# Attention in four in-order queues: output products in high and low parts, q's copy on ScalarE, and steps of VectorE, ScalarE and GpSimd in another order

## The reference

```
x: (16, 512, 256); 16 heads of 64; windows of 128 tokens, 4 in a sequence
qkv = x @ w_qkv;  q, k = l2norm(q) * q_scale * 8, l2norm(k) * k_scale
q, k rotated by position (cos, sin)
each window attends to itself, the one before and the one after
sim = where(mask, -max, q k^T);  attn = softmax(sim);  out = attn v
y = layernorm(x + out @ w_out)
```

## Time and profile before

| | |
|---|---|
| median of 3 runs | 3100.35 us (3098.9 to 3100.77) |
| the profiled execution | 3097.64 us, its span 3095.8 us |
| PE busy | 2941.9 us (95% of the span) |
| DVE busy | 2357.9 us (76%) |
| ACT busy | 2162.1 us (70%) |
| POOL busy | 1662.0 us (54%) |
| masked scores, VectorE, 1024 | 529.7 us |
| exps, ScalarE, 1024 | 572.0 us |
| output products, TensorE, 1024 records | 228.0 us |

### The profile page before, as it was taken

The page is one execution under the profiler, slowest core; times in us unless marked ns, Lnnn a source line. Parts: engine busy times, 40 slices in busy tenths (PEclk is TensorE's granted clock), DMA queues, the critical chain, the costliest instruction groups (busy, mean ns, idle before and its releaser), DMA issues. The chain is left out here.

```text
span 3095.8 us, 60269 instructions
## 1 busy us (share of the span) xinstructions
PE 2941.9 (95%) x20143; PEld 2332.4 (75%) x20143; DVE 2357.9 (76%) x6845; ACT 2162.1 (70%) x5670; POOL 1662.0 (54%) x2226
## 2 busy tenths in 40 slices
PE   7999999999999999999999996799999999999996
PEld 5777777777777777777777774578888888888885
DVE  6877877877877877877877875787777777777775
ACT  5666766766766766766766764577888888888884
POOL 5655655655655655655655654344555555555555
PEclk9999999999999999999999998899999999999998
DMA  2000000000000000000000002100000000000000
GB/s 84 8 15 22 8 15 22 8 15 22 8 15 17 13 15 15 15 15 15 15 15 15 8 21 64 47 15 8 15 15 15 21 20 16 15 15 15 8 15 21
DMA packets 51218, 57.50 MB, mean 19 GB/s; under 512 B 3008, under 2 KB 48592, under 8 KB 50912
## 3 DMA queue, kind: packets, MB, share of 16 engines
q1 hardware_dynamic: 47904, 50.67, 5.1%
q10 hardware_dynamic: 3008, 2.98, 0.3%
HBM read 36.86 MB, written 16.78 MB: 17 GB/s over the span
## 5 line engine op out<-in xcount | busy, mean ns | idle before, releaser
L627 POOL TENSOR_SCALAR a_ex<-a_ex,a_rc 128x384 f32<-128x384 f32 (+1 forms) x1024 | 533.8, 536 | 691.4 <-DVE a_rc L538 691.2
L433 ACT ACTIVATE a_ex<-a_sm,a_nm 128x384 f32<-128x384 f32 (+1 forms) x1024 | 572.0, 560 | 72.5 <-DVE a_nm L531 61.2
L531 DVE CUSTOM_DVE_ANT_0 a_sm<-sc,a_mask,a_rn 128x384 f32<-128x384 f32 (+1 forms) x1024 | 529.7, 543 | 6.3 <-PE sc L303 6.3
L439 ACT ACTIVATE a_pt<-tp 128x256 f32<-128x256 f32 (+1 forms) x512 | 220.1, 430 | 290.5 <-PE tp L322 290.5
L267 PE MATMUL pj<-a_whi,a_xhi 128*128 128x384 f32 x1024 | 390.3, 381 | 8.8 <-DVE a_wlo L187 5.8
L1695 POOL TENSOR_TENSOR b_alo<-b_ring,b_ahi 128x512 fp32r<-128x512 f32 x128 | 169.6, 1325 | 411.7 <-DVE b_ring L1524 388.0
L611 POOL TENSOR_TENSOR a_qr<-a_ra,a_rb 128x256 f32<-128x256 f32 x512 | 370.5, 739 | 11.2 <-DVE a_rb L511 8.4
L267 PE MATMUL pj<-a_whi,a_xlo 128*128 128x384 f32 x1024 | 347.4, 339 | 0.0
L267 PE MATMUL pj<-a_wlo,a_xhi 128*128 128x384 f32 x1024 | 346.3, 338 | 0.0
L331 PE MATMUL qk<-a_pt,a_v 128*64 128x384 f32 (+1 forms) x2048 | 303.9, 437 | 29.0 <-DVE a_pt L543 26.8
L303 PE MATMUL sc<-a_kT,a_qT 64*64 64x256 f32 (+1 forms) x4096 | 307.6, 415 | 1.6 <-DVE a_nm L531 0.9
(11 more groups left out here) (234 smaller groups left out, 7988.7 us busy)
## 6 DMA issues: line engine op xcount, KB each, us to landing
a_xres<-x SPq DMA_DIRECT2D x16, 512.0 KB, 3.8
y<-a_res SPq DMA_DIRECT2D x16, 512.0 KB, 2.9
b_y<-y SPq DMA_DIRECT2D x16, 512.0 KB, 3.8
a_xin<-x SPq DMA_DIRECT2D x15, 512.0 KB, 3.8
out<-b_y SPq DMA_DIRECT2D x15, 512.0 KB, 2.9
a_xin<-wqkv SPq DMA_DIRECT2D x8, 256.0 KB, 2.7
a_ot<-wqkv ACTq DMA_DIRECT2D x3, 384.0 KB, 9.8
a_stage<-wqkv SPq DMA_DIRECT2D x3, 384.0 KB, 12.3
```

What stands on the lines that cost most here:

```text
L433: e.activation(ex[h][w][:, 0:width], sm[h][w % 2][:, 0:width], ACT.Exp, bias=nm[:, w, h:h + 1], scale=-1.0, accum_out=rs[:, w, h:h + 1]).t ...
L439: e.activation(pt_window(0, w), blocks(TP, w), ACT.Copy).then_inc(g['pt_act'], 1)
L531: e.tensor_tensor_reduce(out=sm[h][w % 2][:, 0:width], in0=SC[w % 2][h][:, 0:width], in1=mem['mask'][:, off:off + width], scale=rn[:, par, ...
L627: e.tensor_scalar(row, row, 0.0, rc[:, w, h:h + 1], ALU.add, ALU.mult).then_inc(g['exn_pool'], 1)
```

## The change

The transposed output of attention, `ot`, and its weights `wo` (fp32) become pairs of a high and a low part in the type fp32r: `ohi` is ScalarE's copy of the value products, `olo` is VectorE's difference between these and `ohi`; `wo_hi` and `wo_lo` are made in the first sequence. Each output product becomes three. TensorE's q transposes, which overwrite the bank, wait for `olo`. q's copy goes from VectorE to ScalarE. Masked scores are written straight to `ex`. On TensorE, q's transposes come after the first weights' transposes and half of a projection, and k's after those of window 1's first head. On VectorE, in half u = 1 of pairs 1 to 5 and 7, the last copy of weights and the rotation of chunk 2 come ahead of the last masked score, and the reciprocal of window 1 goes into the next half, behind the rotation of chunk 3. The second statistics go to the end of (1, 0), the power to the end of (1, 1). The residual's x is loaded into `res` itself, so that transfer waits for the maxima and the store. The diff, cut to its core:

```diff
@@ pe_q_transpose, pe_k_transpose, pe_transpose_weights (h and spare)
-            e.wait_ge(g['ot_act'], n)
+            e.wait_ge(g['ol_dve'], n)
-        e.wait_ge(g['qt_dve'], m + 1)
+        e.wait_ge(g['qt_act'], m + 1)
@@ pe_values
-        e.wait_ge(g['pt_act'], NW * n + NW)
-        e.wait_ge(g['pt_dve'], NW * n + NW)
         for k in range(NW):
+            if k in (0, 2):
+                e.wait_ge(g['pt_act'], NW * n + NW - 1 + k // 2)
+                e.wait_ge(g['pt_dve'], NW * n + (NW if k or spare(NW * n + NW - 1) else NW - 1))
@@ pe_out_project
             for c in range(HC):
-                last = e.matmul(QK[:, t * DIM:(t + 1) * DIM], ot[:, c, ...],
-                    wo[:, c, :], start=c == 0, stop=c == HC - 1)
+                for j, (rows_t, weight) in enumerate(((ohi, wo_hi), (olo, wo_hi), (ohi, wo_lo))):
+                    last = e.matmul(QK[:, t * DIM:(t + 1) * DIM], rows_t[:, c, tokens], weight[:, c, :],
+                        start=c == 0 and j == 0, stop=c == HC - 1 and j == 2)
@@ pe_half, u == 0
-            if at.has_pair(1):
-                pe_q_transpose(e, n, n + 1, (p + 1) % 2)
             pe_transpose_weights(e, i, w, 0, at.has_next())
             if at.has_pair(2):
                 pe_project(e, seq, n + 2, pair, w, 0)
+            if at.has_pair(1):
+                pe_q_transpose(e, n, n + 1, (p + 1) % 2)
+            if at.has_pair(2):
                 pe_project(e, seq, n + 2, pair, w, 1)
             pe_transpose_weights(e, i, w, 1, at.has_next())
+            pe_transpose_weights(e, i + 1, w + 1, 0, at.has_next())
             if at.has_pair(1):
                 pe_k_transpose(e, n + 1, (p + 1) % 2)
-            pe_transpose_weights(e, i + 1, w + 1, 0, at.has_next())
@@ act_half, u == 0
+            act_evacuate_weights(e, i, w)
             if ahead:
                 act_exp(e, next_i, next_w, 0)
-            act_evacuate_weights(e, i, w)
+            if at.has_pair(1):
+                act_q_evacuate(e, n + 1, (p + 1) % 2)
             if ahead:
                 act_exp(e, next_i, next_w, 1)
                 act_exp(e, next_i + 1, next_w + 1, 0)
             if at.has_pair(2):
                 act_project(e, n + 2, (p + 2) % PAIRS, w)
+            act_evacuate_weights(e, i + 1, w + 1)
             if at.has_pair(1):
                 act_k_evacuate(e, n + 1, (p + 1) % 2)
-            act_evacuate_weights(e, i + 1, w + 1)
@@ act_half, u == 1
                 act_exp(e, next_i, next_w, 0)
+            if at.has_pair(2):
+                act_project(e, n + 2, (p + 2) % PAIRS, w)
...
                 act_exp(e, next_i + 1, next_w + 1, 1)
-            if at.has_pair(2):
-                act_project(e, n + 2, (p + 2) % PAIRS, w)
+        if at.first and (at.at(3, 1) or at.at(5, 1)):
+            act_out_weights(e, p // 4)
@@ new on VectorE
+    def dve_o_low(e, n, p):
+        e.wait_ge(g['ot_act'], n + 1)
+        e.tensor_tensor(olo[:, p, :], QK[:, :], ohi[:, p, :].bitcast(F32), ALU.subtract).then_inc(g['ol_dve'], 1)
@@ dve_half
             dve_rotate(e, n + 1, 3)
+        if u == 0 and i and spare(i - 1):
+            dve_reciprocals(e, i + 1, w + 1)
+        if u == 0 and at.has_pair(1):
             dve_norms(e, n + 1)
         if u == 1 and at.has_pair(2):
             dve_rotate(e, n + 2, 1)
-        if not at.first:
-            if at.at(1, 0):
-                dve_stats(e, at.b - 1, 1)
+        if u == 0 and at.has_pair(-1):
+            dve_o_low(e, n - 1, (p - 1) % PAIRS)
...
-        if u == 0 and at.has_pair(1):
-            dve_q_evacuate(e, n + 1, (p + 1) % 2)
...
         dve_evacuate_weights(e, i, w)
+        if ahead and u == 1 and spare(i + 1):
+            dve_evacuate_weights(e, i + 1, w + 1)
+            if at.has_pair(2):
+                dve_rotate(e, n + 2, w)
+            dve_mask_max(e, next_i + 1, par, next_w + 1, 1)
+            dve_reciprocals(e, next_i, next_w)
+        else:
+            (as before: masked score, reciprocal, statistics and residual, copy;
+             then for u == 0 the rotation ahead of the second reciprocal)
+        if at.at(1, 0) and not at.first:
+            dve_stats(e, at.b - 1, 1)
@@ pool_half
             pool_rotate(e, n + 2, p % 2, w)
-        if at.at(1, 0) and not at.first:
+        if at.at(1, 1) and not at.first:
             norm.rstd(e, at.b - 1)
+        if at.first and p in (4, 6):
+            pool_out_weights(e, p // 6, u)
@@ SP
             def keep(seq):
-                e.wait_ge(g['op_dve'], 2 * seq)
-                e.dma_start(mem['xres'][:, :, :], x_tiles[seq]).then_inc(g['x_keep'], 16)
+                if seq:
+                    e.wait_ge(g['am_dve'], seq)
+                    e.wait_ge(g['y_out'], 16 * seq)
+                else:
+                    e.wait_ge(g['wo_pool'], 4)
+                e.dma_start(mem['res'][:, :, :], x_tiles[seq]).then_inc(g['x_keep'], 16)
             for b in range(B - 2):
                 load(b + 2)
+                store(b)
                 keep(b + 1)
-                store(b)
```

More of the change, by code:

```diff
@@ L167, in run_attention, with dma_out_weights, act_out_weights, pool_out_weights @@
     w_in = [nc.alloc_semaphore(f'att_w_in{k}') for k in range(len(PIECES))]
-    w_raw = [mem['stage'][:, :], flat(mem['ot'])[:, 0:3 * HD]]
+    w_raw = [mem['raw'][:, c, :] for c in range(DC)]
     def piece_columns(k):
         return slice(PIECES[k][0] * 3 * PW, (PIECES[k][-1] + 1) * 3 * PW)
-    RAW_UNDER = {0: 3, 3: 4, 4: 5}
+    wo_raw = flat(mem['res'])
+    wo_split = [t[:, :, :].rearrange('p c n -> p (c n)') for t in (wo_hi, wo_lo)]
+    def dma_out_weights(e, k):
+        e.dma_start(mem['res'][:, :, :], io['wo0'].rearrange('(c p) n -> p c n', p=P)[:,
+            4 * k:4 * k + 4, :]).then_inc(g['wo_in'], 16)
+    def act_out_weights(e, k):
+        e.wait_ge(g['wo_in'], 16 * (k + 1))
+        e.activation(wo_split[0][:, k * 1024:(k + 1) * 1024], wo_raw, ACT.Copy).then_inc(g['wo_act'], 1)
+    def pool_out_weights(e, k, part):
+        e.wait_ge(g['wo_act'], k + 1)
+        cols = slice(k * 1024 + part * 512, k * 1024 + (part + 1) * 512)
+        e.tensor_tensor(wo_split[1][:, cols], wo_raw[:, part * 512:(part + 1) * 512],
+            wo_split[0][:, cols].bitcast(F32), ALU.subtract).then_inc(g['wo_pool'], 1)
     x_first = [nc.alloc_semaphore(f'att_x_first{k}') for k in range(2)]
@@ L486, in act_half @@
                 act_exp(e, next_i, next_w, 0)
+            if at.has_pair(2):
+                act_project(e, n + 2, (p + 2) % PAIRS, w)
+            if ahead:
                 act_exp(e, next_i, next_w, 1)
@@ L528, in dve_mask_max @@
         e.wait_ge(g['sc_pe'], 2 * i + h + 1)
-        if due(2 * i + h - 3):
-            e.wait_ge(g['e_act'], 2 * i + h - 3)
-        e.tensor_tensor_reduce(out=sm[h][w % 2][:, 0:width], in0=SC[w % 2][h][:, 0:width],
+        e.tensor_tensor_reduce(out=ex[h][w][:, 0:width], in0=SC[w % 2][h][:, 0:width],
             in1=mem['mask'][:, off:off + width], scale=rn[:, par,
@@ L560, in dve_amax @@
         col = TT * seq + t
-        e.tensor_reduce(mem['amax'][:, col:col + 1], mem['res'][:, t, :], AX.X, ALU.max, apply_absolute_value=True)
+        last = e.tensor_reduce(mem['amax'][:, col:col + 1], mem['res'][:, t, :], AX.X, ALU.max,
+            apply_absolute_value=True)
+        if t == TT - 1:
+            last.then_inc(g['am_dve'], 1)
     def dve_half(e, at):
@@ L680, in _ @@
                 e.wait_ge(signal, 16 * DC)
-            e.dma_start(mem['wo'][:, :, :], io['wo0'].rearrange('(c p) n -> p c n', p=P)).then_inc(g['wo_in'], 16)
-            e.dma_start(mem['xres'][:, :, :], x_tiles[0]).then_inc(g['x_keep'], 16)
             load(1)
+            e.wait_ge(g['trig_dve'], 1)
+            dma_out_weights(e, 0)
+            e.wait_ge(g['wo_pool'], 2)
+            dma_out_weights(e, 1)
+            keep(0)
             for b in range(B - 2):
                 load(b + 2)
+                store(b)
                 keep(b + 1)
-                store(b)
-            keep(B - 1)
-            store(B - 2)
             e.wait_ge(g['xt_pe'], 2 * B)
@@ L692, in _ @@
             for k in range(W1_COUNT):
+                if k == 2:
+                    store(B - 2)
+                    keep(B - 1)
                 if k >= 2:
@@ L736, in _ @@
             act_norms(e, 0, 0)
-            for t in range(TT - 1):
+            for t in range(2):
                 act_project(e, 1, 1, t)
+            act_q_evacuate(e, 0, 0)
+            act_project(e, 1, 1, 2)
             act_k_evacuate(e, 0, 0)
@@ L805, in attention_memory @@
         rc=[P, NW, 2], **Norm.buffers('ln1')).items()}
+    with ExitStack() as first:
+        mem['raw'] = first.enter_context(nc.sbuf_tensor('a_raw', [P, DC, 3 * HD], F32))
+    mem['ohi'], mem['olo'] = (sb(k, [P, PAIRS, S], F32R) for k in ('ohi', 'olo'))
+    mem['wo_hi'], mem['wo_lo'] = (sb(k, [P, HC, DIM], F32R) for k in ('wo_hi', 'wo_lo'))
     mem['whi'], mem['wlo'] = (sb(k, [P, DC, 3 * HD], F32R) for k in ('whi', 'wlo'))
```

65 lines of the change are left out of this document (34 added, 31 removed).

## The result

| kernel | median us | lowest to highest | ratio, 95% interval |
|---|---|---|---|
| before | 3098.9 | 3097.95 to 3100.77 | |
| after | 3275.27 | 3271.45 to 3277.7 | 1.0564 [1.0549, 1.0578] |

The change makes the kernel 5.6% slower. The forecast was 3228 with a range to 3270: the direction, the place and most of the size were right, and 47 us were missing. The profiled execution after has a span of 3274.9 us, 179.1 above that of before, where the sum had 128.

A forecast was written before the change was run, and what follows sets the result against it. No queue is full; four in-order queues hand work round per pair of heads. Fifteen sequences +119, first +5, last calls -2.6, low rows +0.7, clock +4.5, start +1: together +128, so 3228 us, range 3130 to 3270.

The forecast's parts named there:

- The chain of the ordinary pair: From value products' start V: late masked score, exp, rotation, reciprocal, normalisations, additions; q transposes 1.4 us late, pair 13.7.
- The chain of pair 2: Power behind normalisations delays norm, output copy and low rows; q transposes 5.3 us late, pair 17.7 against 12.63.
- Pair 0: Interval holding the output products: 26.21 - 2.6 + 1.4 - 0.2 = 24.8 us.
- The output products: On TensorE, 0.119 us a step; saves 1.3 a call, 2.6 a sequence, 42 us over 32 calls.
- Rivals 1, 2, 4 and 5: 1 only norm holds, 3139 (0.10); 2 only pairs stretch, 3163 (0.10); 4 faster, 3058 or 3031 (0.11); 5 draw (0.03).
- Pair 7: Follows a pair without the moved reciprocal; only low rows ahead of the scores delay it: 13.3 us, against 12.42.
- the moved reciprocal: VectorE's reciprocal of window 1 behind chunk 3's rotation, ending V+3.21; GpSimd's normalisations and additions wait for it.
- Pair 1: Stays at 13.5 us: the wait for q's copy goes, statistics move behind.
- I take 0.3 us for each of 15 sequences: TensorE's half clock after pair 2's gap: 0.3 us a sequence, ends 0 and 1.7; +4.5 in the sum.
- rival 3: The clock at full price in pair 2: +1.4 x 15 on the forecast, 3249 us; chance 0.12.
- pair 6: Stall as in ordinary pairs, x's transposes (0.5) and an order of its own: 14.3 us.
- First and last sequence: First: pairs 2 to 7 +0.9 each, +5, and +1 for splitting output weights; last priced like a steady sequence.

The follow-up runs named there:

- e2: Changed kernel, with 26 unused TensorE products put into pair 2's wait for the low rows, output unchanged: 3249.74 us, 1.0490 of before.
- e6: e5 with ScalarE's copies of chunk 2 in the second half again behind the exps: 3107.25 us, 1.0024 of before.
- e5: Changed kernel with the power ahead of the normalisations, and VectorE's second-half order and both reciprocals as before: 3120.6 us, 1.0070 of before.
- e7: e6 with q's copy back on VectorE, behind the second masked score: 3095.5 us, 0.9991 of before.
- e9: e7 without VectorE's low rows, high rows used twice instead, so the output is not the layer's: 3070.92 us, 0.9907 of before.
- e3: Changed kernel with only window 1's reciprocal back, right after window 0's as VectorE's last step of the half: 3240.19 us, 1.0460 of before.
- e12: e7 with ScalarE's first-half order of before, and the sums of squares of q and k in two parts: 3079.34 us, 0.9936 of before.
- e1: Changed kernel with GpSimd's power for the norm ahead of the softmax normalisations in half (1, 1): 3186.17 us, 1.0288 of before.

## Why the prediction was right in kind and 47 us short

**Right.** The chain of the ordinary pair: forecast masked score V+0.41, reciprocal V+3.04 to V+3.21 less overlaps (V+2.9), q transposes V+5.6; found V+0.09, V+2.59, V+5.43. Pairs 3 and 4 at 13.7 are 13.65. The chain of pair 2: power over at V+6.3, q transposes V+9.5; found V+6.08, V+9.55; without the clock's part it lasts 18.07 (e2), 17.7 forecast. Pair 0: 24.8, found 25.19. The output products: 0.119 a step, found 0.120. Rivals 1, 2, 4 and 5 are out.

**Right number, wrong reason.** Pair 7, 13.3 against 13.48, was put on the low rows; e6 shows ScalarE's early copies of chunk 2, which I had passed over, as 1.05 of it: TensorE waits 0.55 for the low rows there after, 0.53 in e5 and not at all in e6. With those copies back, leaving the low rows out changes pair 7 by 0.01 (e7 to e9). And the prediction blamed the moved reciprocal in ordinary pairs: e3 shows that moving it back alone gives nothing there. What counts is that the masked score stands behind the rotation, from which two chains run, through GpSimd and through VectorE's own sums and low rows. Pair 1, 13.5 against 13.57, was to stay because the wait for q's copy goes. It goes (0.64 before), but the moved statistics now stand ahead of the rotation and the masked scores of the second half, and TensorE waits 0.93 for one of these. Timelines of VectorE and TensorE in pair 1 after, V at 945.91:

```profile
954.41 0.73 DVE L66 BATCH_NORM_STATS2 a_ln_bn<-a_res 128x6 f32<-128x256 f32 x2
...
957.53 0.52 PE L339 MATMUL sc<-s_ident,a_ex 128*128 128x128 f32 x3 [0.93 <-DVE a_nm L561]
```

This wait is in every changed kernel down to e12, whose pair 1 is 13.97 against 13.53 before; no experiment puts the statistics back.

**Wrong: "I take 0.3 us for each of 15 sequences".** This term, the clock, is the step that failed most: the mechanism was named, its size was four times too small. e2 gives the clock's price as 0.83 and 1.88 in turn, 1.35 on average, some 1.05 x 15 = 16 us more. It is rival 3, +1.4, given 0.12. I took the one stretch of the earlier trace rows to fall into waiting, while the row after shows the 0.50 from V+7.9 to V+14.7 of pair 2: it begins 1.65 before the q transposes and covers the work behind them. The Trainium skill, "TensorE: Matmul & The Clock Gate", section "Why this matters for your kernels", says to leave no idle gaps of some us between bursts of matmuls; e1 and e2, one with a gap of 1.16 in place of 5.16 and one with the gap filled, agree, with no stretch at 0.50 in their steady sequences.

**Sizes off in the steady sequence.** Pair 2's wait +0.4, pair 6 (14.94, some 14.3 forecast) +0.6, pair 0 +0.4, pair 7 +0.2, less 0.1 in the others: 1.5 x 15 = 22 us. Pair 0's 0.4 is as much as the output products fell short, which saved 2.2 and not 2.6. In pair 6 the wait ahead of the q transposes is not larger than elsewhere (1.09 against 1.03 in pair 3); between e1 and e5 VectorE's order takes 1.1 off it, which is as far as the runs go.

**First and last sequence.** +12.0 and +15.0, where 6 and 8.2 were forecast. In both GpSimd also subtracts weights, the output's in the first and the next layer's in the last; I had counted the first at 1 us and the others at nothing. In the last sequence, timelines of GpSimd after, then of TensorE before and after, at pair 6:

```profile
2052.28 0.72 POOL L653 TENSOR_TENSOR a_qr<-a_ra,a_rb 128x256 f32<-128x256 f32 x1
2052.97 1.27 POOL L673 TENSOR_TENSOR s_w_lo<-a_xin,s_w_hi 128x512 fp32r<-128x512 f32 x1
2054.21 0.71 POOL L653 TENSOR_TENSOR a_qr<-a_ra,a_rb 128x256 f32<-128x256 f32 x1
...
1879.12 0.66 PE L278 MATMUL qk<-s_ident,a_qr 128*128 128x128 f32 x4 [0.88 <-POOL a_qr L611]
...
2054.97 0.66 PE L295 MATMUL qk<-s_ident,a_qr 128*128 128x128 f32 x4 [3.29 <-POOL a_qr L653]
```

The 1.27 for the next layer's weights, in the kernel before too, stands between the additions that the q transposes wait for. GpSimd's chain already ended last there before, by 0.88; with the late reciprocal in front of it the wait is 3.29, in e3 1.93, in e5 0.81. With the reciprocal alone put back (e3) the last sequence falls from 128.18 to 121.57 and the first from 107.49 to 104.27; with e5 to 112.96 and 100.06, against 113.19 and 95.49 before.

The clock, which I had priced in pair 2 alone, has a part in this too. The windows view after, in pairs 5 and 6 of the last sequence:

```profile
2039.16:2042.58 3.42, 3.42 (x17) 3.34 (x16) 1.42 (x6) 3.39 (x12) 1.33 (x3) 0.50 0.11 40
2056.23:2063.06 6.83, 5.97 (x31) 3.66 (x31) 3.44 (x14) 4.17 (x14) 3.33 (x5) 0.50 0.12 31
```

Two more such stretches of 3.4 us lie in pairs 4 and 6 of the first sequence. Neither before nor e5 has one in these pairs. What the clock costs of the 12.0 and 15.0 no run separates. Of the 4.6 that e5 leaves in the first sequence e6 and e7 give back 3.0 and e12 another 1.1 (95.98), all with the output weights' split in place, so the split costs little there.

The claim that on SP no transfer is held up stands: the third piece of the next layer's weights is behind a store and the transfer of x, but is issued at 2029.85, when GpSimd's first subtraction of those weights (2028.54, 1.28 long) ends, and the transfer of x had gone at 2027.19. Behind the last V the saved 2.6 of the products is not found: 1202.0 against 1199.7. The changed kernel and its variants spread from 1196.1 to 1202.0 there, nearly all with the same code in that part, so I leave it open.

On the profiled executions the sum was 51 us short (179 against 128): 16 for the clock, 22 for the sizes, 4 for the last sequence beyond a steady one, 6 for the first and 4 behind the last V make 52.

## What to carry to other kernels

In in-order queues price a reordering by the chain it puts in front of the engine that sets the period, and follow every queue that the late result passes: putting the reciprocal of 0.2 us back gave nothing in ordinary pairs and took 1.0 off pair 2's wait (e3), while putting the power's 1.3 us back took 5 to 6 us off pair 2 (e1), by what stood behind each. When two chains leave one late instruction, putting one of them right shows nothing (e3), so test the common start. A change of many edits can hold one good core: taking the power out from behind the normalisations and undoing VectorE's order, ScalarE's third chunk and q's copy gave back 180 us, and what was left, with the sums in halves, is 20 faster than before.

## What the runs showed of the hardware

The same 5 us gap of TensorE, repeated every sequence, brought stretches at 0.50 of 3.4 and 6.8 us in turn (the windows above: 18.90 and 19.92 for the same work), so a loss by the clock can have two sizes within one kernel. In e2, 26 products a sequence that compute nothing took this loss away and delayed nothing: pair 2 is 18.07 and 18.09, and its q transposes start at V+9.54, after V+9.55.
